# Preparing the second stage beside the first, and identity products in five waits

## The reference

```
x = layernorm(x + A(x))   # Taylor terms + gated feed-forward, hidden 1248
x = layernorm(x + B(x))   # gated feed-forward with LoRA, hidden 1376
x = layernorm(x + C(x))   # state space block (Mamba2), 128 heads
x = layernorm(x + D(x))   # gated feed-forward with ternary weights, hidden 2048

A: up = x @ up_w.T; delta = x @ gate_w.T - point
   out = up @ local.T + sum over m = 1..6 of (delta**m / m! * up, cut off above 4) @ fuse[m].T
         + (silu(x @ g.T) * (x @ u.T)) @ d.T
B: every weight w is w + 2 * lora_B @ lora_A, rank 16
```

## Time and profile before

| | us |
|---|---|
| median of 3 runs | 2260.9 (2256.44 to 2263.07) |
| the profiled execution | 2260.12 |
| its span | 2258.3 |
| TensorE busy | 2120.7 (94%) |
| VectorE busy | 1728.2 (77%) |
| ScalarE busy | 1231.6 (55%) |
| GpSimd busy | 690.5 (31%) |
| mean granted clock of TensorE | 0.968 |

### The profile page before, as it was taken

The page is one execution under the profiler, slowest core; times in us unless marked ns, Lnnn a source line. Parts: engine busy times, 40 slices in busy tenths (PEclk is TensorE's granted clock), DMA queues, the critical chain, the costliest instruction groups (busy, mean ns, idle before and its releaser), DMA issues. The chain is left out here.

```text
span 2258.3 us, 35600 instructions
## 1 busy us (share of the span) xinstructions
PE 2120.7 (94%) x10769; PEld 1698.0 (75%) x10833; DVE 1728.2 (77%) x2942; ACT 1231.6 (55%) x2207; POOL 690.5 (31%) x418
## 2 busy tenths in 40 slices
PE   7999589978989999999999999999999999988997
PEld 6787478867867777777777777777777777766876
DVE  6444355547868889888888888888888888888886
ACT  2112113434357676776767767777776776763232
POOL 5544044421113324323333332333333323331000
PEclk9999789989999999999999999999999999998999
DMA  4211241313232212221221221221222122112433
GB/s 159 98 43 61 85 137 57 112 55 80 94 108 76 66 62 68 70 66 56 66 80 48 75 80 47 75 80 47 64 76 62 56 80 66 56 52 80 140 126 112
DMA packets 126019, 176.39 MB, mean 78 GB/s; under 512 B 17669, under 2 KB 83717, under 8 KB 125317
## 3 DMA queue, kind: packets, MB, share of 16 engines
q1 hardware_dynamic: 125892, 175.07, 24.7%
HBM read 165.72 MB, written 9.31 MB: 78 GB/s over the span
## 5 line engine op out<-in xcount | busy, mean ns | idle before, releaser
L72 PE MATMUL bank<-xT_hi,C_w_hi 128*128 128x512 f32 x1160 | 477.6, 412 | 16.0 <-POOL C_w_lo L1522 9.1
L73 PE MATMUL bank<-xT_lo,C_w_hi 128*128 128x512 f32 x1160 | 463.6, 400 | 0.0
L74 PE MATMUL bank<-xT_hi,C_w_lo 128*128 128x512 f32 x1160 | 463.2, 399 | 0.0
L1522 POOL TENSOR_TENSOR C_w_lo<-C_raw,C_w_hi 128x512 fp32r<-128x512 f32 x130 | 184.3, 1418 | 779.6 <-ACT C_w_hi L1616 734.2
L1229 DVE SCALAR_TENSOR_TENSOR C_acc<-bank,C_par,C_acc 128x510 f32<-128x510 f32 (+2 forms) x384 | 281.2, 745 | 53.2 <-ACT C_acc L1576 30.5
L1345 DVE TENSOR_TENSOR C_decay<-C_decay,C_cb 128x512 f32<-128x512 f32 x384 | 291.1, 786 | 4.8 <-ACT C_decay L1702 4.8
L72 PEld LDWEIGHTS bank<-xT_hi,C_w_hi 128*128 128x128 f32 x1160 | 223.1, 192 | 71.2 <-POOL C_w_lo L1522 10.4
L74 PEld LDWEIGHTS bank<-xT_hi,C_w_lo 128*128 128x128 f32 x1160 | 222.4, 192 | 52.4
L73 PEld LDWEIGHTS bank<-xT_lo,C_w_hi 128*128 128x128 f32 x1160 | 223.6, 193 | 46.0
L1326 DVE TENSOR_TENSOR C_group_out<-bank,C_group_out 128x512 f32<-128x512 f32 x184 | 126.4, 687 | 111.4 <-PE bank L74 111.4
L72 PE MATMUL bank<-C_out_hi,C_yg_hi 128*128 128x512 f32 x512 | 201.4, 393 | 7.3 <-DVE C_yg_lo L1315 4.9
(11 more groups left out here) (263 smaller groups left out, 4416.8 us busy)
## 6 DMA issues: line engine op xcount, KB each, us to landing
C_raw<-in_Cxg SPq DMA_DIRECT2D x65, 512.0 KB, 3.6
C_cs_second<-cs_rows SPq DMA_DIRECT2D x64, 512.0 KB, 4.6
C_raw_out<-in_Cout SPq DMA_DIRECT2D x64, 256.0 KB, 2.9
ahead_raw<-in_D SPq DMA_DIRECT2D x32, 512.0 KB, 3.6
A_raw<-in_A SPq DMA_DIRECT2D x20, 512.0 KB, 3.6
B_right_raw<-in_D SPq DMA_DIRECT2D x16, 512.0 KB, 3.6
ahead_raw<-in_D SPq DMA_DIRECT2D x32, 256.0 KB, 2.6
cb_rows<-C_decay SPq DMA_DIRECT2D x8, 768.0 KB, 3.2
```

Source lines behind the costliest of these rows:

```text
L72: pe.matmul(out, lh, rh, start=start, stop=False)
L73: pe.matmul(out, lh, rl, start=False, stop=False)
L74: return pe.matmul(out, ll, rh, start=False, stop=stop)
L1522: e.tensor_tensor(w_lo[:, slot, :], raw_at, f32(w_hi[:, slot, :]), ALU.subtract).then_inc(lo_done, 1)
```

## The change

Seven edits.

1. Start of A: the Taylor weights are loaded ahead of the second half of x; only the first half is transposed before the Taylor products, the second behind them (into banks 0 to 3 again). Their low part moves from VectorE to GpSimd. The high part of the fuse weights moves to ScalarE, the low part is split over tiles 0 to 2.
2. The powers and terms on GpSimd are spread over five tiles of each half (`TERMS`) instead of two.
3. A class `Front` holds the buffers and semaphores that A fills for B. The LoRA pack is loaded in seven chunks into the free Taylor buffer and split beside A's tiles; B's tiles 0 and 1 are loaded into A's weight buffers behind A's last tiles; the folds and splits of both are done at the end of A.
4. A's second-half norm isn't computed at A's end but in B's first pass (`early`), with the transposes behind `down` (`late`).
5. The start of B with loads, packing and folds of two tiles is gone.
6. `keep_busy`: 8 products of the identity with itself at the start, 8 at the end of A, 12 ahead of the transposes at the end of B, 10 at the start of C, 12 ahead of the transposes at the end of C.
7. In C, in the unit that gets a group's mean squares, the first `in_g` stands ahead of the second `seg`.

```diff
+def keep_busy(pe, sh, out, count):
+    for _ in range(count):
+        pe.matmul(out[:, 0:P], sh.ident[:, :], sh.ident[:, :], start=True, stop=True)
...
+class Front:
...
+        beside = ((0, 2), (0, 5), (0, 8), (1, 2))
+        right = [("right", self.right, slice(w * i, w * (i + 1)), slice(64, 96), beside[i]) for i in range(4)]
+        m = 2 * D + B_PAD // 2
+        return right + [("left", self.left, slice(0, 2 * D), slice(32, 64), (1, 5)),
+                        ("left", self.left, slice(2 * D, m), slice(32, 64), (1, 8)),
+                        ("left", self.left, slice(m, self.LW), slice(32, 64), (1, 9))]
...
-        early = HalfNorm(sh, ctx, f"{kind}_in", 1) if kind == "D" else None
+        early = HalfNorm(sh, ctx, f"{kind}_in", 1) if kind != "A" else None
...
-                sp.dma_start(sh.ident[:, :], sh.ident_dram).then_inc(x0_in[0], 16)
+                sp.dma_start(sh.ident[:, :], sh.ident_dram).then_inc(ident_in, 16)
                 sp.dma_start(sh.x[:, 0:HT, :], A["x"][:, 0:HT, :]).then_inc(x0_in[0], 16)
+                sp.dma_start(tay_raw[:, :], A["tay"]).then_inc(tay_in, 16)
                 sp.dma_start(sh.x[:, HT:TT, :], A["x"][:, HT:TT, :]).then_inc(x0_in[1], 16)
-                sp.dma_start(tay_raw[:, :], A["tay"]).then_inc(tay_in, 16)
...
+            LORA_AT = ((0, 2), (0, 5), (0, 8), (1, 1), (1, 5), (1, 8), (1, 9))
+            def load_lora(c):
+                name, _, cols, _, _ = front.chunks()[c]
+                if c == 0:
+                    sp.wait_ge(tay_ready, 1)
+                else:
+                    sp.wait_ge(packed, c)
+                sp.dma_start(tay_raw[0:LORA_ROWS, 0:cols.stop - cols.start], A[name][:, cols]).then_inc(front.lora_in, 16)
+            def load_front():
+                for n in range(2):
+                    sp.wait_ge(free13, 2 * TL - 1 + n)
+                    sp.dma_start(raw13[:, n, :], A["B13"][n, :, :]).then_inc(front.raw13_in[n], 16)
+                    sp.wait_ge(free2, 2 * TL - 1 + n)
+                    sp.dma_start(raw2[:, n, :], A["B2"][n, :, :]).then_inc(front.raw2_in[n], 16)
...
+            def lora_low(c):
+                _, tile, cols, rows, _ = front.chunks()[c]
+                v.wait_ge(packed_hi, c + 1)
+                v.tensor_tensor(tile[rows, cols], tay_raw[rows, 0:cols.stop - cols.start], f32(tile[rows, cols]),
+                                ALU.subtract).then_inc(packed, 1)
+            def front_tiles():
+                for n in range(2):
+                    fold13(n, n)
+                    v.wait_ge(fold_done, 2 * n + 2)
+                    v.wait_ge(up_mm, 2 * TL - 1 + n)
+                    v.tensor_scalar(w13h[:, n, :], raw13[:, n, :], 1.0, None, ALU.mult).then_inc(front.w13_hi, 1)
+                for n in range(2):
+                    fold2(n, n)
+                v.wait_ge(fold2_done, 1)
+                v.wait_ge(down_mm, 2 * TL - 1)
+                v.tensor_scalar(w2h[:, 0, :], raw2[:, 0, :], 1.0, None, ALU.mult).then_inc(front.w2_hi, 1)
...
                 for_tiles(v, TL, body)
+            if kind == "A":
+                front_tiles()
             half_sum(1)
+            if kind == "A":
+                return
...
+                g.wait_ge(tay_hi, 1)
+                g.tensor_tensor(tay_l[:, :], tay_raw[:, :], f32(tay_h[:, :]), ALU.subtract).then_inc(tay_ready, 1)
...
+        TERMS = (((), (1, 2), (3,), (4,), (5,), (6,)), ((1, 2), (3,), (4,), (5,), (6,), ()))
-                        for m in (range(1, 4), range(4, ORDERS + 1))[n]:
+                        for m in TERMS[hf][n]:
...
+                        x0_high(1)
+                        a.wait_ge(fuse_in, 16)
+                        a.activation(fuse_h[:, :, :], fuse_raw[:, :, :], ACT.Copy).then_inc(tay_hi, 1)
...
+                pe.wait_ge(ident_in, 16)
+                keep_busy(pe, sh, sh.bank[4], 8)
+                x0_turn(0)
                 pe.wait_ge(x0_ready, KT)
                 pe.wait_ge(tay_ready, 1)
-            if kind == "B":
-                pe.wait_ge(packed, 3)
-                fold_up(0, 0)
-                fold_up(1, 1)
-                pe.wait_ge(packed, 5)
-                fold_down(0, 0)
-                fold_down(1, 1)
-                pe.wait_ge(fold2_done, 2)
...
                         down(hf, n - 1, 1 - par, isinstance(n, int) and n == 1, False)
+                    if turns and late:
+                        pe.wait_ge(fold2_done, n + 2)
+                        for k in (2 * n - 8, 2 * n - 7):
+                            nm.turn(pe, k, turn_bank(hf, n, k))
...
                         fold_up(n + 2, par)
+                    if turns and late:
+                        pe.wait_ge(nm.x_ready, 2 * n - 6)
...
                     for m in range(ORDERS + 1):
+                        if hf and m == 3:
+                            pe.wait_ge(packed, 5)
+                            pe.wait_ge(hid_done, 2 * TL)
+                            fold_up(0, 0)
+                            fold_up(1, 1)
...
+                    if hf:
+                        fold_down(0, 0)
+                        fold_down(1, 1)
                 down(hf, TL - 1, (TL - 1) % 2, False, True)
-            if kind != "D":
+            if kind == "A":
+                pe.wait_ge(fold_done, 4)
+                keep_busy(pe, sh, sh.bank[5], 8)
+            if kind == "B":
+                keep_busy(pe, sh, sh.bank[4], 12)
                 for k in range(KT):
                     norms[1].turn(pe, k, sh.bank[k])
...
+            keep_busy(pe, sh, bank[7], 10)
             pe.wait_ge(S.dtw_lo, 1)
...
                 if not u.first:
                     seg(u, 0)
+                    if not u.group_ended:
+                        seg(u, 1)
+                in_g(u, 0)
+                if u.group_ended:
                     seg(u, 1)
-                in_g(u, 0)
                 in_g(u, 1)
...
+            pe.wait_ge(norm.summed, 1)
+            keep_busy(pe, sh, bank[TAIL_BANK[0]], 12)
             for k in range(KT):
                 norm.turn(pe, k, bank[TAIL_BANK[k]])
```

More of the change, by code:

```diff
@@ L370, in load @@
                         sp.dma_start(fuse_raw[:, :, :], A["fuse"]).then_inc(fuse_in, 16)
+                    if kind == "A" and isinstance(n, int):
+                        if (hf, n) == (1, TL - 1):
+                            load_front()
+                        for c in range(Front.PACKED):
+                            if LORA_AT[c] == (hf, n):
+                                load_lora(c)
                 for_tiles(sp, TL, load)
@@ L397, in feed_forward, with turns_late, lora_beside @@
         TURNS = (4, 5)
+        def turns_late(hf):
+            return kind == "B" and hf == 0
+        def lora_beside(hf, n):
+            return [c for c in range(Front.PACKED) if kind == "A" and isinstance(n, int)
+                    and front.chunks()[c][4] == (hf, n)]
+        TERMS = (((), (1, 2), (3,), (4,), (5,), (6,)), ((1, 2), (3,), (4,), (5,), (6,), ()))
         def norm_step(hf, n):
@@ L432, in norm_begins, with late_turns @@
                     nm.invert(v)
-                elif n in TURNS and not (kind == "D" and hf):
+                elif n in TURNS and not (kind == "D" and hf) and not turns_late(hf):
                     for k in (2 * n - 8, 2 * n - 7):
                         nm.low(v, k, turn_bank(hf, n, k))
+            def late_turns(hf, n):
+                if turns_late(hf) and n in TURNS:
+                    for k in (2 * n - 8, 2 * n - 7):
+                        early.low(v, k, turn_bank(hf, n, k))
             def norm_ends(hf, n):
@@ L744, in _ @@
                 for_tiles(g, TL, body)
+            if kind == "A":
+                for n in range(2):
+                    g.wait_ge(front.w13_hi, n + 1)
+                    g.tensor_tensor(w13l[:, n, :], raw13[:, n, :], f32(w13h[:, n, :]), ALU.subtract)\
+                     .then_inc(front.w13_ready, 1)
+                g.wait_ge(front.w2_hi, 1)
+                g.tensor_tensor(w2l[:, 0, :], raw2[:, 0, :], f32(w2h[:, 0, :]), ALU.subtract).then_inc(front.w2_ready, 1)
         @block.scalar
@@ L821, in body @@
                         a2_copy(n + 2)
+                    late_turns(hf, n)
+                    for c in lora_beside(hf, n) if not split_last(hf, n) else ():
+                        lora_high(c)
                     for i, slot in size_tiles(hf, n, par) if kind == "B" else ():
@@ L947, in body @@
                     nm = in_pass[hf] if isinstance(n, int) and not (kind == "D" and hf) else None
+                    late = turns_late(hf)
                     turns = nm is not None and n in TURNS
-                    if turns:
+                    if turns and not late:
                         pe.wait_ge(hid_done, n + hf * TL)
```

259 lines of the change are left out of this document (139 added, 120 removed).

## The result

| | before | after |
|---|---|---|
| median | 2258.7 us (2255.3 to 2263.1) | 2189.1 us (2187.5 to 2191.0) |
| the profiled execution | 2260.12 | 2190.99 |
| its span | 2258.3 | 2188.9 |

The ratio is 0.9691, with a 95% interval of 0.967 to 0.9712: 69.5 us less, against 69.8 forecast. Both medians are of four runs.

A forecast was written before the change was run, and what follows sets the result against it. TensorE, busy 2120.7 of 2258.3 us, was the bound; other engines matter only where it waits or runs slow. Seven places summed to -69.8 from 2260.1, giving 2190 us (2182 to 2198 at chance 0.57); range 2174 to 2215.

The forecast's parts named there:

- term 3: From A to B: packing done beside A, B's second tile at 266.1 instead of 300.5, -34.4 us; bounds -28, -37.
- Term 6: Group ends in C: mean-square waits covered (-9.1) and 6.9 of 9.5 us slow products regained, -16 us; bounds 0, -18.6.
- Term 1: Start of A: Taylor weights arrive earlier, first gate product at 19.7 instead of 26.99, -7.3 us; bounds -3.5, -9.
- Term 2: Two stalls in A on GpSimd's late low parts go when its work is spread: -6.3 and -6.4 us; bounds -12.7, 0.
- Rival C: In A, VectorE and GpSimd hold each other up and the two stalls only spread: 2203 us, chance 0.10.
- near 258: Sign at the start of B: its first gate product near 258 of the span, no wait before it over 3 us.
- Rival D: End of A: B's preparation ends behind A's last product, 8 to 14 us lost: 2200, about 2204 at most; chance 0.07.
- E: Slower: A's weight loads stand behind chunk loads in SP's queue; 11.2 us per miss, 2268 if all seven; chance 0.02.
- Term 4: B's first pass gets A's second-half norm: transposes and waits cost 2 us per tile at two tiles, +4.0; bounds +2, +8.
- Term 5: From B to C: identity products fill waits, faster turns (-1.0) and first 24 products (-1.2), -2.2 us; bounds +0.5, -4.
- Term 7: From C to D: twelve identity products in the wait of 5.0 us make the turns faster, -1.2 us; bounds 0, -3.
- Rival B: Start, B, seams and C: identity products too short, clock not held, 15.6 us less gain: 2206 us; chance 0.17.

The follow-up runs named there:

- the repeat: The changed kernel run once more with no edit, as yardstick for the kernels on the same chip: 2189.6 us, ratio 0.9685.
- the second series of the products alone: The kernel before with only identity products added (start, end of A, C's seams), run a second time: 2274.2 us, ratio 1.0061.

## Why the prediction was right, step by step

The forecast was 2190, the median is 2189.1. The terms against the traces (1 to 3 share one landmark: A's last product moved by -16.9. Only this sum is measured. It is split here as -7.3 for the start, -12.7 for the stalls, as forecast and as the kernel with that edit alone has it within 0.1, and the +3.1 that are left for the folds; the 3.1 belong to term 3, -37.5 + 3.1 = -34.4. Term 6 runs up to the last unit's decay products, at 2017.68 before and 1948.36 after):

```
                               forecast   measured
1 start                          -7.3       -7.3
2 two stalls in A               -12.7      -12.7
3 A to B                        -34.4      -34.4
4 norm in B's first pass         +4.0       +4.9
5 B to C                         -2.2       -1.5
  C's opening                     0         +0.4
6 group ends in C               -16        -18.8
7 C to D, and D                  -1.2       -0.1
```

**Term 1.** The first Taylor product came at 11.18 (11.4 forecast) and the 24 products took 5.86 (6.5). The first gate product is 8.4 earlier, but tile 1 waits 1.10 for the low part of x, a wait that was not foreseen. The sum is right because these two cancel, which is luck. The load order is worth 3.4 us of it at the end of A, in one trace, and the slow Taylor products of that trace are part of them.

**Term 2.** Right within 0.1, and shown by itself. GpSimd's tile fits into 8.34 us of TensorE. Rival C's mechanism is there but doesn't reach the path: VectorE's rounding of a tile takes 1.70 us beside GpSimd (0.70 for as many columns free of it; 2.89 were read the earlier trace rows), and no product waits for it. The row of after (timeline of VectorE):

```profile
49.84 1.70 DVE L561 TENSOR_SCALAR front_w13h<-front_raw 128x1024 fp32r<-128x1024 f32 x1
```

**Term 3.** From A's last product to B's second tile -37.5 was forecast and -37.5 came. B's first gate product stands at 238.4; "near 258" counted on the time line of before, where the 20.0 us won in A (7.3, 12.7) are not yet taken off: 238.4 + 20.0 = 258.4. B was not late: the one wait before it is 1.10 us, behind the identity products. That its first product comes 2.89 us behind A's last, where 2.8 was put in, is luck in part. VectorE's sums end 0.74 behind A's last product and not 1.6, and without identity products B's first product comes 1.91 behind; they do not end beside the sums, as forecast, but 1.04 us behind them, and make up the rest. Rival D is out, and so is E: no product waits for a weight tile in A. Half of the whole gain lies here, and the edit (points 3 to 5 of the change) was not run by itself; its size rests on the two traces, which don't separate the preparation of B from the norm moved into it.

**Term 4.** +4.9 lies in the bounds. Two tiles wait 0.73 and 0.91 and the turns take 1.09 each where 0.9 was put in.

**Term 5.** The -1.0 for the turns did not come. Twelve products end at 443.15 and 3.16 us of wait follow; the turns then ran at 0.56, 3.39 us against 3.62. With 24 products they take 1.97. What was mis-sized is the cover: 2.6 us of products were known to stand in a wait of 5.8, and the rest of the wait was counted as if it did no harm. Such a cover isn't always too short, only not dependable: with the same 12 products and the same wait the turns took 3.56 us in the repeat and 1.97 in the second series of the products alone. C's 72 products gained 1.4 where 1.2 was put in.

**Term 6.** Forecast -16, by taking 6.9 of 9.5 us of clock; -18.8 came, the 9.1 of waits and all of the clock. Nothing else moved up. At these places the clock goes with the wait, and the discount of 2.6 was too careful. The seven places take 8.05 us each after, from the sum to the first output product, where they took 9.4 to 12.5.

**Term 7.** The turns went from 3.68 to 1.97 us, in this profile; in the repeat they took 2.96. Before them, at C's last unit, 1.2 us were lost, in a stretch that nobody touched (22.77 us from the decay products to C's last against 21.57; 21.50 in the repeat), and the clock is low there. Windows of after, from the last unit's decay products on:

```profile
1948.30:1955.40 7.10, 4.48 (x34) 3.19 (x35) 4.67 (x7) 1.45 (x2) 5.71 (x3) 0.74 0.01 3
1955.40:1962.70 7.30, 7.29 (x28) 6.14 (x29) 4.79 (x7) 2.23 (x3) 2.37 (x1) 0.59 0.00 0
```

The measured terms add up to -69.5; the spans differ by 69.4. That the forecast comes within 1 us is luck: terms 4 to 7 and C's opening are off by +0.9, +0.7, -2.8, +1.1 and +0.4 and add up to 0.3. The mechanisms of the three large terms, 2, 3 and 6, are right; the small ones are of the size of what changes from one run to the next.

**The rule on the clock.** The Trainium skill, "TensorE: Matmul & The Clock Gate", section "PE-mode transpose", says that transposes don't count as activity. Two kernels here don't agree: 2187.8 and 2184.4 us with transposes, against 2189.6 and 2185.5 with products. In the trace of before, where TensorE had nothing but 16 transposes from 489.9 on, the clock rose at their end; in the kernel without identity products it stayed low behind the same 16. First two windows of before, then two of that kernel:

```profile
495.73:499.10 3.37, 3.37 (x16) 3.28 (x16) 1.38 (x2) 1.70 (x3) 0.00 (x0) 0.50 0.00 0
499.20:502.50 3.30, 0.15 (x1) 0.00 (x0) 1.38 (x2) 0.60 (x1) 0.00 (x0) 1.00 0.00 0
```

```profile
445.80:449.47 3.67, 3.67 (x16) 3.27 (x16) 1.57 (x3) 1.79 (x3) 0.00 (x0) 0.50 0.00 0
449.50:456.30 6.80, 0.00 (x0) 0.00 (x0) 1.94 (x4) 0.60 (x1) 1.26 (x1) 0.50 0.54 127
```

So the clock can rise behind transposes alone and doesn't always; what decides is not shown.

**The chances.** Rival B, the clock not held, came true in the turns of one seam, at about the 1.0 us credited there. It put 8.7 us on the identity products' places (3.8, 1.5, 2.2 and 1.2); the kernel without them lost 1.5. They are worth that much of 69.5, and the clock came back mostly without them. Of the signs, the first gate product of A came at 18.55 ("near 20"), C shrank by 19.6 us, from first product of C to first of D, and the clock was 1.00 behind all seven sums of squares.

## What to carry over

A wait costs its length and then a slow stretch; at C's group ends, taking the wait away by order also brought the clock back. Fill only waits that can't be removed, and not where the next product could start; fill them whole, since a half-filled wait gave full speed in one profile and next to nothing in another. Before a term is credited, lay the two time lines on each other and look at which wait comes right behind. And before a us at a seam is put down to an edit, look at the same seam in kernels that don't have the edit.

## What was not expected of the hardware

- Products added at the seams alone made the kernel before 8 and 16 us slower (2269.7 and 2274.2 us, against 2262.0 and 2258.4); its profiles show stalls of TensorE of 5.2 to 5.9 us, 640 us or more behind the last of these products that stand ahead of them, with eight or nine more packets of instructions for each. The same helper in the changed kernel brings none. With the stretches that hold stalls put at 172.5 us, the two profiles would lie 5 and 3 us below the kernel before, so by this estimate the stalls hide a small gain. Which of the places brings the stalls, and by what rule, stays open; the eight at the start alone do not.
- In C's opening, from the end of the 72 products to the first sum of squares, the same code took 306.2 to 306.6 us in three kernels (the change, its repeat, without products) and 303.2 to 303.4 in three others (the load order, both with more products); the seventh profile of this form, with transposes, took 304.8 and the kernel before 305.8. The wait of 3.30 us is the same in all; the 24 products behind it take from 5.85 to 8.55 us. Such a level changes with what happens elsewhere, so a median that moves by 3 us is no proof of an edit: its place in the span is.
- The granted clock reads 1.00 in the first 10 us of the span, but 16 records of identity products take 3.78 us there and the same 16 take 1.95 at the end of A. The reading says nothing there: the trace of after has no record of the clock before 8.9 us (that without identity products none before 14.9), and a stretch without a record reads as 1.00.
